# AdaLN block on one core: last stage unrolled, three residual buffers, split up-projection in one run

## What is computed

```
h = layernorm(x) * (1 + ca) + sa
x = x + ga * attention(h)                 # ends in: out @ Wo.T + bo
h = layernorm(x) * (1 + cb) + sb
logits = h @ router_w.T                   # 4 experts, the best 2 kept, softmax over them
mid = einsum('tf,erf->ter', h, A)         # 4 experts of rank 16
x = x + gb * sum_e gates_e * (mid_e @ B_e.T) * 4
```

## Time and profile before

| | |
|---|---|
| median of 3 runs | 3138.91 us (3135.16 to 3140.53) |
| profiled execution | 3136.15 us |
| its span, first to last instruction | 3134.2 us |
| mean granted clock of PE | 0.958 |
| busy: PE, DVE, ACT, POOL | 2896.5, 1470.5, 1043.1, 1375.4 us |
| `finish`, first DMA to the end | 2492.53 to 3134.2 us |

### The profile page before, as it was taken

The page is one execution under the profiler, slowest core; times in us unless marked ns, Lnnn a source line. Parts: engine busy times, 40 slices in busy tenths (PEclk is TensorE's granted clock), DMA queues, the critical chain, the costliest instruction groups (busy, mean ns, idle before and its releaser), DMA issues. The chain is left out here.

```text
span 3134.2 us, 46142 instructions
## 1 busy us (share of the span) xinstructions
PE 2896.5 (92%) x16692; PEld 2042.1 (65%) x16692; DVE 1470.5 (47%) x3029; ACT 1043.1 (33%) x1442; POOL 1375.4 (44%) x701
## 2 busy tenths in 40 slices
PE   3999899989998999699999999999999769999997
PEld 1888788868887888455555555555555456677775
DVE  4121221131212111466666666666666356666664
ACT  1222321222122111155555555555555411112111
POOL 2221322242224111277767777777677513333332
PEclk7999999999999999699999999999999879999997
DMA  6444342333323543735544445554444254434431
GB/s 229 175 165 157 127 161 107 134 134 134 134 107 124 192 167 147 159 91 125 120 109 113 109 111 124 125 123 113 113 109 109 70 173 119 121 107 133 138 105 54
DMA packets 149741, 404.89 MB, mean 129 GB/s; under 512 B 17356, under 2 KB 52612, under 8 KB 148568
## 3 DMA queue, kind: packets, MB, share of 16 engines
q1 hardware_dynamic: 119272, 292.83, 27.7%
q10 hardware_dynamic: 30320, 110.15, 15.8%
HBM read 271.20 MB, written 131.20 MB: 128 GB/s over the span
## 5 line engine op out<-in xcount | busy, mean ns | idle before, releaser
L907 ACT ACTIVATE prob<-ps_s 128x1024 f32<-128x1024 f32 (+3 forms) x768 | 597.5, 811 | 498.2 <-PE ps_s L1029 425.1
L610 PE MATMUL ps_u<-h_hi,w_hi 128*128 128x512 f32 x1536 | 603.6, 393 | 0.0
L425 POOL TENSOR_TENSOR w_lo<-w_raw,w_hi 128x1024 fp32r<-128x1024 f32 x96 | 231.0, 2407 | 842.5 <-ACT w_hi L472 842.5
L610 PE MATMUL ps_u<-h_lo,w_hi 128*128 128x512 f32 x1536 | 599.1, 390 | 0.0
L610 PE MATMUL ps_u<-h_hi,w_lo 128*128 128x512 f32 x1536 | 598.8, 390 | 0.0
L863 POOL TENSOR_TENSOR added<-added,prob 128x2048 f32<-128x2048 f32 (+1 forms) x128 | 550.3, 4299 | 11.0 <-ACT prob L907 10.7
L999 PE MATMUL ps_r<-k_st,q_st 96*128 96x512 f32 (+2 forms) x1536 | 499.2, 381 | 42.3 <-DMA v_sb<-v_tok 27.7
L1029 PE MATMUL ps_s<-q_st,k_st 97*128 97x512 f32 (+2 forms) x1536 | 458.0, 380 | 28.0 <-ACT prob L907 22.7
L547 DVE SCALAR_TENSOR_TENSOR qk_lo<-ps_u,bias_col,qk_hi 128x512 fp32r<-128x512 f32 x128 | 96.1, 751 | 671.9 <-ACT qk_hi L448 671.9
L999 PEld LDWEIGHTS ps_r<-k_st,q_st 96*128 96x128 f32 x1536 | 273.4, 193 | 204.1 <-issue 68.0
L951 DVE TENSOR_REDUCE part_high<-ps_r 128x1 f32<-128x512 f32 x512 | 340.3, 685 | 96.5 <-PE ps_r L999 87.8
(11 more groups left out here) (159 smaller groups left out, 3006.1 us busy)
## 6 DMA issues: line engine op xcount, KB each, us to landing
q_st<-qk_split ACTq DMA_DIRECT2D x90, 512.0 KB, 7.6
k_st<-qk_split ACTq DMA_DIRECT2D x90, 512.0 KB, 13.8
w_raw<-w_cols SPq DMA_DIRECT2D x72, 512.0 KB, 3.5
qk_split<-qk_hi SPq DMA_DIRECT2D x64, 512.0 KB, 2.6
qk_split<-qk_lo SPq DMA_DIRECT2D x64, 512.0 KB, 3.4
xn<-in_L_attn_x SPq DMA_DIRECT2D x8, 2048.0 KB, 12.5
v_tok<-v_out SPq DMA_DIRECT2D x32, 512.0 KB, 2.7
wm<-in_L_wmod SPq DMA_DIRECT2D x8, 2048.0 KB, 9.1
```

The source lines that it names most:

```text
L425: nc.gpsimd.tensor_tensor(w_lo[:, m], w_raw[:, m], w_hi[:, m].bitcast(F32), ALU.subtract).then_inc(w_lo_done, 1)
L610: last = nc.tensor.matmul(ps_u[u % 2][:], w[:, m, k], h[:, k, tok], start=k == 0 and j == 0, stop=k == KT - 1 and j == 2)
L907: nc.scalar.activation(prob[:, buffer_of(t, k), 2 * pair:2 * pair + 2, off:], ps_s[pair][:, :, off:], ACT.Exp, scale=SCALE).then_inc(exp_d ...
```

## The change

In `prepare` the small weight `up_t` is loaded and turned twice, side by side, so that it fills 128 partitions. In `finish` all 16 chunks are straight code. There are three residual buffers; `att_y` has two slots for four. The store of a chunk is two DMAs, one for each token tile. The up-projection is split: `up_hi` and `up_lo` hold the weight and its remainder as fp32r, `mid_s` holds `mid` as a value and its remainder, and each of the four units is two fp32r matmuls, one of 128 rows and one of 64. The orders are new: `go_up` of chunk n-1 is one run of four units behind the second projection unit of chunk n+1, and the turns of chunk n come behind that run; on DVE the four deltas of chunk n-1 come behind the second residual, and `gates` of chunk n behind the first layer norm; POOL adds chunk n-1 ahead of `at_lo` of chunk n+2; SP issues the attention loads, two half stores and the residual in that order.

```diff
-        up_t = keep("up_t", [ER, D])
+        up_t = keep("up_t", [2 * ER, D])
-        up_in = sb("up_in", [P, KT, ER])
+        up_in = sb("up_in", [P, KT, 2, ER])
             for e in range(E):
-                sp.dma_start(up_in[:, :, e * R:(e + 1) * R], lb[e]).then_inc(small_loaded, 16)
+                for copy in range(2):
+                    sp.dma_start(up_in[:, :, copy, e * R:(e + 1) * R], lb[e]).then_inc(small_loaded, 16)
-                nc.tensor.transpose(ps_small[0:ER, P:2 * P], up_in[:, k], ident[:]).then_inc(small_done, 1)
+                nc.tensor.transpose(ps_small[:, P:2 * P], up_in[:, k].rearrange("p c r -> p (c r)"), ident[:]).then_inc(small_done, 1)
...
+    RES = 3
-        res = [sb(f"res{i}", [P, T, D]) for i in range(2)]
+        res = [sb(f"res{i}", [P, T, D]) for i in range(RES)]
+        up_lo = nc.alloc_sbuf_tensor_at("up_lo", [ER, D], F32R, offset=shared)
+        up_hi = sb("up_hi", [2 * ER, D], F32R)
-        att_y = sb("att_y", [P, UN, BANK])
+        att_y = sb("att_y", [P, HV, BANK])
-        mid_t = sb("mid_t", [ER, CW])
+        mid_s = sb("mid_s", [P, T, 2, ER], F32R)
+        mid_t = sb("mid_t", [2 * ER, CW], F32R)
-        wo_in += [att_y[:, i * HV:(i + 1) * HV].rearrange("p a b -> p (a b)") for i in range(T)]
+        wo_in += [res[RES - 1][:, i] for i in range(T)]
...
-            def chunk(b, i, last):
-                n = b * CPB + i
-                if not (last and i + 3 >= CPB):
-                    wait_apart(sp, at_lo_done, n + 3, tally)
-                    load_at(b, i + 3)
-                wait_apart(sp, out_ready, T * (n + 1), tally)
-                sp.dma_start(tokens(out, b, i), delta[:]).then_inc(out_stored, 16)
-                if not (last and i + 2 >= CPB):
-                    load_res(b, i + 2)
...
+            sp.wait_ge(wo_turned, KT)
+            load_res(2)
+            for n in range(NC + 1):
+                if n + 3 < NC:
+                    sp.wait_ge(at_lo_done, n + 3)
+                    load_at(n + 3)
+                if n > 0:
+                    for a in range(T):
+                        sp.wait_ge(out_ready, T * (n - 1) + a + 1)
+                        sp.dma_start(tokens(out, n - 1, a), delta[:, a]).then_inc(out_stored[a], 16)
+                    if n + 2 < NC:
+                        load_res(n + 2)
+                    if n % CPB == 0 and batch_of(n) + 1 < NB:
+                        load_gates(batch_of(n) + 1)
...
+            for n in range(NC + 1):
+                if n > 0:
+                    for a in range(T):
+                        add_residual(n - 1, a)
+                if n + 2 < NC:
+                    split_lo(n + 2)
+                if n + 1 < NC:
+                    for a in range(T):
+                        rsqrt(n + 1, a)
...
+            nc.scalar.copy(up_hi[:], up_t[:]).then_inc(up_hi_done, 1)
...
+                lora = down[:, :, 0:ER].rearrange("p t (e r) -> p t e r", e=E)
+                share = gate[:].unsqueeze(3).to_broadcast([P, T, E, R])
+                nc.vector.tensor_tensor(mid[:].rearrange("p t (e r) -> p t e r", e=E), lora, share, ALU.mult).then_inc(mid_whole, 1)
+                nc.vector.tensor_tensor(mid_s[:, :, 0].rearrange("p t (e r) -> p t e r", e=E), lora, share, ALU.mult).then_inc(mid_whole, 1)
+                dve.wait_ge(mid_whole, 2 * (n + 1))
+                nc.vector.tensor_tensor(mid_s[:, :, 1], mid[:], mid_s[:, :, 0].bitcast(F32), ALU.subtract).then_inc(mid_ready, 1)
...
+            dve.wait_ge(inv_stored, 16 * NB)
+            dve.wait_ge(up_hi_done, 1)
+            nc.vector.tensor_tensor(up_lo[:], up_t[0:ER], up_hi[0:ER].bitcast(F32), ALU.subtract).then_inc(up_lo_done, 1)
...
+            for n in range(NC):
+                ahead = n + 1 < NC
+                if n + 2 < NC:
+                    divide(n + 2)
+                if ahead:
+                    residual(n + 1, 0)
+                if n > 0:
+                    keep_mid(n - 1)
+                if ahead:
+                    residual(n + 1, 1)
+                if n > 0:
+                    experts(n - 1, range(UN))
+                if ahead:
+                    residual(n + 1, 2)
+                    layernorm(n + 1, 0)
+                gates(n)
+                if ahead:
+                    residual(n + 1, 3)
+                    layernorm(n + 1, 1)
+            keep_mid(NC - 1)
+            experts(NC - 1, range(UN))
...
-                    nc.tensor.matmul(ps_d[u % 2], mid_t[:, a * P:(a + 1) * P], up_t[:, hv * BANK:(hv + 1) * BANK], start=True, stop=True).then_inc(d_done, 1)
+                    nc.tensor.matmul(ps_d[u % 2], mid_t[:, tok], up_hi[:, cols], start=True, stop=False)
+                    nc.tensor.matmul(ps_d[u % 2], mid_t[0:ER, tok], up_lo[:, cols], start=False, stop=True).then_inc(d_done, 1)
...
-                for u, other in enumerate((turn, go_down, turn_mid, go_up)):
-                    if ahead:
-                        project(b, i + 1, u)
-                    other(n)
...
+            for n in range(NC):
+                ahead = n + 1 < NC
+                if ahead:
+                    project(n + 1, 0)
+                if n > 0:
+                    turn_mid(n - 1)
+                if ahead:
+                    project(n + 1, 1)
+                if n > 0:
+                    go_up(n - 1, range(UN))
+                turn(n)
+                if ahead:
+                    project(n + 1, 2)
+                go_down(n)
+                if ahead:
+                    project(n + 1, 3)
+            turn_mid(NC - 1)
+            go_up(NC - 1, range(UN))
```

More of the change, by code:

```diff
@@ L1184, in finish, with batch_of, tokens @@
         block = ctx.enter_context(nc.Block())
[L1186 to L1196, removed]
+        def batch_of(n):
+            return n // CPB
+        def tokens(a, n, t):
+            return a[n // CPB, (n % CPB) * CW + t * P:(n % CPB) * CW + (t + 1) * P, :]
@@ L1299, in _ @@
-            for i in range(2):
-                split_lo(0, i)
-            for a in range(T):
-                rsqrt(0, 0, a)
-            def chunk(b, i, last):
-                n = b * CPB + i
-                if not (last and i + 2 >= CPB):
-                    split_lo(b, i + 2)
-                for a in range(T):
-                    if not (last and i == CPB - 1):
-                        rsqrt(b, i + 1, a)
-                    pool.wait_ge(d_free, UN * n + HV * (a + 1) + 2)
-                    nc.gpsimd.tensor_tensor(delta[:, a], delta[:, a], res[i % 2][:, a], ALU.add).then_inc(out_ready, 1)
@@ L1314, in _, with split_lo, rsqrt, add_residual @@
-            chunks(pool, chunk)
+            def split_lo(n):
+                pool.wait_ge(at_hi_done, n + 1)
+                nc.gpsimd.tensor_tensor(at_lo[n % 2][:], at_raw[:], at_hi[n % 2][:].bitcast(F32), ALU.subtract).then_inc(at_lo_done, 1)
+            def rsqrt(n, a):
+                pool.wait_ge(var_ready, T * n + a + 1)
+                nc.gpsimd.tensor_tensor(rstd[:, a:a + 1], mean_var[:, a, 1:2], minus_half[:], ALU.pow).then_inc(rstd_ready, 1)
+            def add_residual(n, a):
+                pool.wait_ge(d_free, UN * n + HV * (a + 1))
+                nc.gpsimd.tensor_tensor(delta[:, a], delta[:, a], res[n % RES][:, a], ALU.add).then_inc(out_ready, 1)
@@ L1344, in chunk @@
                         nc.scalar.activation(h2t[:, k], ps_t[q % TB][:, j * CW:(j + 1) * CW], ACT.Identity,
-                                             bias=cols[:, b, 0, k:k + 1], scale=cols[:, b, 1, k:k + 1]).then_inc(h2_ready, 1)
-                if not (last and i + 2 >= CPB):
-                    split_hi(b, i + 2)
+                                             bias=cols[:, batch_of(n), 0, k:k + 1], scale=cols[:, batch_of(n), 1, k:k + 1]).then_inc(h2_ready, 1)
+                if n + 2 < NC:
+                    split_hi(n + 2)
@@ L1447, in _ @@
                     nc.vector.reciprocal(inv[:, 1:], inv[:, 1:]).then_inc(inv_ready, 1)
[L1448 removed]
+                divide(i)
                 if i == 0:
@@ L1548, in _ @@
             for u in range(1, UN):
-                project(0, 0, u)
-            def chunk(b, i, last):
-                n = b * CPB + i
-                ahead = not (last and i == CPB - 1)
-                for u, other in enumerate((turn, go_down, turn_mid, go_up)):
-                    if ahead:
-                        project(b, i + 1, u)
-                    other(n)
-            chunks(pe, chunk)
+                project(0, u)
+            pe.wait_ge(up_lo_done, 1)
+            for n in range(NC):
+                ahead = n + 1 < NC
[15 more added lines that the diff above has]
+            go_up(NC - 1, range(UN))
 _INS = ["L0_attn_x", "L0_attn_Wq", "L0_attn_bq", "L0_attn_Wk", "L0_attn_bk", "L0_attn_Wv", "L0_attn_bv", "L0_attn_Wo",
```

199 lines of the change are left out of this document (83 added, 116 removed).

## The result

The changed kernel takes **3155.68 us** (median of 5 runs, 3151.05 to 3156.22), the kernel before 3138.91 (5 runs, 3133.26 to 3140.73): a ratio of 1.0054, 95% interval 1.0040 to 1.0069. It is slower by 17 us; 3138 was forecast, and the range ended at 3155.

What follows compares the result with a forecast made beforehand. It took a ring through VectorE, GpSimd and the DMA queue, not TensorE, to bound the kernel. Terms 3.6-8.3+9.5-3.5 = +1.3 us on the profiled execution, with the median's offset shared out, gave 3138 us, range 3120 to 3155.

Steps and rivals of the forecast that it cites:

- to P(0,0): Prologue before projection unit 0 of chunk 0: four more up_in load issues delay the wmod loads, +3.6 us (0 to 4.5).
- P(0,0) to P(2,0): First chunks, projection unit 0 of chunk 0 to that of chunk 2: up_lo delays, but waits and an up run go, -8.3.
- P(2,0) to the end of P(15,3): Chunk 2's first projection unit to chunk 15's last: 14 cycles of 36.1 less 2.2, 503.2 against 493.7 us, +9.5.
- tail: After the last projection unit: shorter up-projection but longer gates and a deferred run, -2.3; half the last store, -1.2.
- the residual wait: VectorE's wait for the residual load, 99.3 us over 14 chunks: taken as gone with three buffers, 3 us to spare.
- The ring: New chunk cycle: at_lo's end, VectorE 23.9, up unit, then turns, ScalarE and at_lo; 35.3 us full clock, 36.5 half.
- the multiplication: VectorE's residual multiplication behind P(n+1,2): blocked by GpSimd's at_lo, 2.5 to 3 us long, ending 0.55 after at_lo.
- unit 3 of the run: Last of four up-projection units, two fp32r products: 0.46 us at full clock, 0.85 at half.
- two cycles in three: Share of chunk cycles with TensorE at half clock, giving a mean cycle of 36.1 us between 35.3 and 36.5.
- Full clock in most chunks: Rival for the chunk cycles: TensorE keeps full clock, 35.3 us a cycle, 11 us less, 3127 us; 25%.
- Half clock through P(n+1,2): Rival: half clock lasts through next chunk's projection unit 2, costing 1.8 us a cycle over forecast, 3163 us; 10%.
- The load: Rival: residual wait returns when DMAs queue over 19.5 us after at_lo, 3145 to 3160 us; 5%.

Runs made afterwards that it cites:

- e7: Changed kernel, with GpSimd subtracting only the first 32 of 256 columns of at_lo from chunk 2 on: 3129.0 us.
- e9: Changed kernel with up_lo on 128 rows, in a third order: two projections before the turns, up units in pairs around P(n+1,3), gates last on VectorE: 3096.9 us.
- e10: e9 with its TensorE order kept, deltas spread singly on VectorE, mid_t and divide behind the first residual unit, GpSimd's first residual addition earlier: 3050.1 us.
- e1: Changed kernel with up_lo filled on all 128 partitions, so both products of an up unit have 128-row weight tiles: 3135.1 us.
- e6: Changed kernel with needless products filling TensorE's two pauses, 10 ahead of the mid_t wait and 4 ahead of the third up unit: 3140.2 us.
- e4: Kernel before, with its order and float32 up-projection, only unrolled and with three residual buffers and half stores: 3095.5 us.
- e2: Changed kernel, with its order and three buffers, but the float32 up-projection of before instead of the split: 3155.6 us.

## Why the prediction was wrong

Span against span, by the prediction's own stretches:

| stretch | forecast | measured |
|---|---|---|
| to P(0,0) | +3.6 | +5.5 |
| P(0,0) to P(2,0) | -8.3 | -8.1 |
| P(2,0) to the end of P(15,3) | +9.5 | +23.4 |
| tail | -3.5 | -0.7 |
| sum | +1.3 | +20.1 |

**Right:** the residual wait is gone. The ring is at_lo, VectorE, the up run, turns, ScalarE, at_lo; e7 shows it by taking at_lo out, e9 and e10 by opening it. Piece by piece: at_lo's end to the first delta 22.1 (22.6 forecast), turns to at_lo's end 11.4 (11.6 at half clock), the multiplication 2.07 long and ending 0.56 after at_lo (0.55), waits of TensorE for mid_t of 2.2 (1.7 to 3.5) and for the delta of 1.0 (1 to 2). First chunks: -8.1 for -8.3.

**The step that failed** is a term's size: "Then unit 3 of the run, as two fp32r products: a unit of 24 takes 5.49, so 0.46", and 0.85 at half clock. A unit takes 0.85 at full clock and 1.45 at half, because its two weight tiles differ in rows. From the first delta to the turns the forecast had 2.35 us at half clock, and it is 3.6 (2.6 in e1, with equal rows): +1.3 a cycle, less 0.5 and 0.2 in the other two pieces, so 37.1 instead of 36.5. The tail holds the same error: eight products of 0.725 are 5.8 us for the forecast's 3.4. e1 puts it right and is at 3135, 3 us from the 3138 forecast. The value came from the nearest row in kind, fp32r products of equal tiles, and was given no upper end, though a row had one: the float32 up unit, 7.19/4 = 1.8 at half clock.

**A second, smaller error** is the share of half clock: "two cycles in three", and it was 12 or 13 of 14, which takes away the 0.4 that the mix had been below 36.5. Both together are 1.0 a cycle over the forecast and 14 of the 19 us that were missed; the tail is 2.8.

**The rest**, 1.9 us before P(0,0), seems to lie in stages that the change leaves alone. The start itself moved by 3.2 us where 3.6 was forecast (TensorE waits for wmod at 33.09 instead of 29.87). From the first stage's first projection to the Wo turns the other profiles took 2414.0 to 2418.4 us, the one of before 2413.1. The changed kernel's took 2416.1. So this looks like the scatter of that part, with the forecast made against its quickest profile.

**The rivals.** Full clock in most chunks did not come; e6 shows it worth 1.6 us a cycle. Half clock through P(n+1,2) did not come: the clock is 1.00 from 2878.70. The load did not come back. The outcome beyond +0.2% was given 25%, but for other reasons.

**What the prediction didn't ask** was whether the order had to be paid at all. It took the wait's 7 us and the new serial 11 us as one bargain; e4 has the third buffer and none of the new order, and is 60 us faster than e2, which differs from it in the orders alone.

## What to carry over

A wait that is taken away is worth what the next chain in the same order leaves, so try the buffer alone before moving work: here -38 us (buffers, straight code and half stores) became +17, for the larger part through an order that puts turns, ScalarE and GpSimd end to end with VectorE's work. Give each hand-over between engines a unit of other work (the third order), and lay VectorE's SBUF operations beside GpSimd's pauses; then TensorE's own work was the cycle. Take the price of a small matmul from a row with the same neighbours: a split product whose weight tiles changed height cost almost double one with tiles of full height.

## What was not expected of the hardware

- fp32r products of 512 columns whose weight tiles alternate between 128 and 64 rows start 0.425 us apart at full clock and 0.725 at half; with 128 rows throughout 0.23 and 0.43. What differs is when the weight load starts: ahead of the 56 64-row loads of the changed kernel the queue of loads was idle for 18.9 us, ahead of the same loads in e1 for 1.9 (2600 to 3100 us; group, busy us and mean ns, idle before; first the changed kernel, then e1).

```profile
L1534 PEld LDWEIGHTS ps_d<-up_lo,mid_t 64*128 64x128 f32 x56 | 13.3, 238 | 18.9 <-issue 18.9
```

```profile
L1534 PEld LDWEIGHTS ps_d<-up_lo,mid_t 128*128 128x128 f32 x56 | 14.9, 266 | 1.9
```

  The loads of both heights are late in the changed kernel: each starts with its own product (at 2870.07 and 2870.49). In e1 a load starts a product ahead (at 2864.26, where its own begins at 2864.49).

```profile
2870.06 0.19 PEld L1533 LDWEIGHTS ps_d<-up_hi,mid_t 128*128 128x128 f32 x1 [0.24 <-issue]
2870.49 0.18 PEld L1534 LDWEIGHTS ps_d<-up_lo,mid_t 64*128 64x128 f32 x1 [0.24 <-issue]
```

```profile
2864.26 0.19 PEld L1533 LDWEIGHTS ps_d<-up_hi,mid_t 128*128 128x128 f32 x1
```

  The Trainium skill (TensorE: Matmul & The Clock Gate, "LDWEIGHTS (loading the stationary operand)") says that a load's time goes by its columns and not by its rows. The loads agree, 238 and 266 ns on average at mixed clock; that they start later when the row count changes is not in that rule.
- After pauses of 2.2 and 1.0 us the granted clock was 0.50 for 6.8 us, in nearly every cycle. With 14 products of no use in the pauses it stayed at 1.00, and the cycle fell by 1.6 us.
- VectorE's xn, a tensor_scalar with one SBUF tile, took 2.83 instead of 0.81 us beside GpSimd's addition.
